# Spreading a state's C row over the partitions with one bf16 product instead of four fp32 transposes

## The chip, the cores and the metric

The kernel runs on one core of a Trainium2 chip. The metric is the device time of one launch in microseconds (us), the median of several runs. The engines are named as the profile names them: PE (TensorE), DVE (VectorE), ACT (ScalarE), POOL (GpSimd) and SP (SyncE, which here only issues DMAs). PEld is PE's weight load.

## What is computed

A block of two parts over x of shape 4 x 512 x 512: a selective scan (Mamba) gated by x, then a feed-forward part with ternary weights. Only the first part is touched by the change. Its core, per batch:

```
x_dbl = einsum('bdl,ed->bel', x, x_proj_w)
dt_low, Bm, Cm = split(x_dbl, [dt_rank, dt_rank + d_state], axis=1)
def step(state, inp):
    d, b, c, u = inp
    dA = exp(d[..., None] * A)
    state = state * dA + (d * u)[..., None] * b[:, None, :]
    y = einsum('bdn,bn->bd', state, c)
```

There are 16 states n, 512 channels d and 512 time steps l. In the kernel a channel is a partition, so state n of 128 channels is one 128 x 512 tile, and c for state n is one row of 512 numbers that all 128 partitions need: it has to be spread.

## The kernel before

The kernel is written engine by engine, with semaphores by hand; the order of the code of an engine is its order of execution, and a wait holds everything behind it on that engine.

**Prologue.** For each of the 4 batches, `project` and the convolution (`conv_start` on ACT, `taps` on DVE, `conv_sums` on POOL, `silu` on ACT) make u; `x_proj(b)` on PE and `rows_out(b)` on ACT make `rows[b]` (dt_low, B and C as 64 rows of 512, in tiles named zt, szT, zn, zt). SP stores rows 32 to 63 to `bc_rows` in HBM (`store_bc(b)`, L276), from where B rows (and some C rows) come back spread by DMA (`load_b`, L318, and `load_c`, L293). PE also transposes the same rows into `xdT` (`rows_transpose`, copied by `rows_copy` on DVE, L1311). Between these DVE makes sums of the weights (`w_abs`, L1303, and `w_means`, from L1316), statistics of x (`x_stats`, L1307) and one quarter of the ternary weights (`w_ternary(3)`, L1331), for which SP waits before it issues `load_b(0, (0,))`, since both use `b_bc`.

SP's list is fixed too: w_gate, x and w_up (4 MB each), then `store_u(0)`, `store_bc(0)`, `store_u(1)`, `store_bc(1)`, `store_u(2)`, `store_bc(2)`, then the loads of B for batch 0 with `store_u(3)` and pieces of x, then `store_bc(3)`, and so on. All go into one queue.

**Scan.** 16 stages s (4 batches x 4 groups of 128 channels) of 16 states n. For each state ACT makes exp (L1107), POOL makes du times B for two states at once (`times_b`, L850), DVE runs the scan (L1454), and the product with C is made either by POOL, for pairs, from C spread by DMA (`times_c`, L842), or by DVE for the "own" states (`times_c`, L1462), from C spread by PE into the PSUM tile pC (`c_bcast`, L477). PE then adds the product into pY by a transpose (`y_sum`, L483). Stages 0 to 3 have 12 own states each; the later ones 8 or 7. In all there are 133 calls of `c_bcast`, each of four transposes. In stages 4 to 15 the feed-forward of earlier token tiles runs beside the scan: PE's `gate_up` (L552), ACT's silu (L1060), DVE's `times_up` (L1406). In stages 0 to 3 pC has two banks for C, after that one.

**Tail.** After the last scan only the feed-forward of the last tiles is left; PE and ACT alternate there.

Of the kernel before, what the change touches and what calls it, by code (L numbers as in the profile page):

```python
# [6 lines left out]
BF16 = mybir.dt.bfloat16  # L7
# [5 lines left out]
P = 128  # L13
# [10 lines left out]
NPROJ = 64  # L24
BROW = 32
# [68 lines left out]
def by_pe(s, n):  # L94
# [11 lines left out]
    k_const k_acc k_lag2 k_tap k_conv k_u k_px k_xp k_rows k_tr k_xdT k_v k_dt k_st k_zs k_a  # L106
# [18 lines left out]
def build(nc, x, ctxT, g_x, g_f, w_in, w_conv, b_conv, w_xp, w_dt, b_dt, a_log, d_skip, w_gate, w_up, w_down,  # L125
          bc_rows, u_rows, out):
    with ExitStack() as stack:
# [3 lines left out]
        def ps(name, shape, dt=F32):  # L131
            return stack.enter_context(nc.psum_tensor(name, shape, dt))
# [82 lines left out]

        pA = ps("pA", [P, 2, 512])
# [56 lines left out]
        def _(sp):  # L273
            def store_bc(b):
                sp.wait_ge(S["k_rows"], b + 1)
                sp.dma_start(bc_rows[b], rows[b][BROW:NPROJ, :]).then_inc(S[f"c_bst{b}"], 16)  # L276

# [76 lines left out]
            sp.wait_ge(S["c_bst0"], 16)  # L354
# [14 lines left out]
            for b in range(1, BATCH):  # L369
                sp.wait_ge(S[f"c_bst{b}"], 16)  # L370
# [24 lines left out]
        def _(pe):  # L395
# [76 lines left out]
            def c_bcast(s, n):  # L472
                m = own(s).index(n)

                past(pe, S["s_mul"], OWN_AT[s] + m - (1 if s < PLAIN else 0))
                for k in range(NT):
                    mm = pe.transpose(c_bank(s, m)[:, k * P:(k + 1) * P],  # L477
                                      xdT[:, s // NT, k, NS + n:NS + n + 1].to_broadcast([P, P]), ident[:, :])
                mm.then_inc(S["s_cb"], 1)
# [296 lines left out]
        def _(gp):  # L776
# [13 lines left out]

            def conv_sums(first, last):
                for i in range(first, last):
                    gp.wait_ge(S["k_tap"], i + 1)
                    gp.wait_ge(S["k_acc"], 2 * i + 2)
                    gp.tensor_tensor(xc[i % 4][:, 1:L], xc[i % 4][:, 1:L], xb[i % 4][:, 1:L], ALU.add).then_inc(S["k_conv"], 1)  # L795
# [14 lines left out]
            w_round(1)  # L810
            conv_sums(12, 14)
# [3 lines left out]
            w_clip(3)  # L815

# [51 lines left out]
            for c in range(NDB):  # L868
                times_b(0, c)
# [58 lines left out]
        def _(act):  # L928
# [19 lines left out]
            def rows_out(b):  # L948

                act.wait_ge(S["k_xp"], b + 1)  # L950
                if b == 3:
                    act.wait_ge(S["c_bst0"], 16)
                    act.wait_ge(S["k_v"], NT)
                    act.wait_ge(S["k_tr"], 1)
                act.activation(rows[b], pT[:, :], ACT.Identity, bias=one_row[:, :]).then_inc(S["k_rows"], 1)
# [158 lines left out]
            def z_copy(s):  # L1114
                act.wait_ge(S["s_szp"], s + 1)
                past(act, S["s_x1"], s)
                if s == 0:
                    act.wait_ge(S["c_bst1"], 16)
                act.activation(szT[:, :], pT[:, :], ACT.Copy, scale=tgate[:, 0:1]).then_inc(S["s_szT"], 1)
# [22 lines left out]
            for s in range(PLAIN):  # L1142
                for n in range(NS):
                    if s * NS + n + 3 < PLAIN * NS + 2:
                        exponential(s * NS + n + 3)
                    if s == 0 and n == 3:
                        act.wait_ge(S["c_bst2"], 16)
                        act.wait_ge(S["k_xdT"], BATCH)
                        act.wait_ge(S["k_zs"], 4)
                        z_silu(0)  # L1150
                        act.wait_ge(S["c_bst3"], 16)
                        z_silu(1)
# [130 lines left out]
        def _(dve):  # L1283
# [44 lines left out]

            def w_ternary(c):
# [7 lines left out]
            dve.tensor_scalar(a_neg[:, :, :], a_raw[:, :, :], -1.0, None, ALU.mult)  # L1337
            w_abs(0, 0)
            taps(6)
# [5 lines left out]
            w_means(0)  # L1345
            taps(10)
# [6 lines left out]
            taps(14)  # L1353
            rows_copy(2)
# [5 lines left out]
            w_ternary(3)  # L1360
            w_abs(1, 0)
# [3 lines left out]
            w_abs(1, 3)  # L1365
            dve.wait_ge(S["c_ust"], 16 * BATCH)
# [230 lines left out]
```

## Time and profile before

| what | value |
|---|---|
| median of 3 runs | 621.03 us (620.51 to 621.07) |
| span of the profiled execution | 617.3 us |
| what lies around the span (median less span) | 3.7 us |
| DVE, POOL, ACT, PE busy, share of the span | 90%, 82%, 84%, 84% |

The span is from the first instruction to the last one in the profile; the profile gives no time of its own beside it, so the median stands in for it, and the difference of 3.7 us is taken as the same for both kernels. A busy share is an average over prologue, scan and tail, which have different limits.

### The profile page before, as it was taken

The page shows a single profiled execution, that of the slowest core. Times are in us where ns is not written, and L with a number is a line of the kernel's source. Part 1 is how long each engine was busy: PE and PEld are TensorE (multiplying, and loading weights), DVE is VectorE, ACT ScalarE, POOL GpSimd, SP SyncE. Part 2 cuts the span into 40 slices and gives each one's busy share as a digit, 9 for nine tenths or more (in the row PEclk, how much of TensorE's full clock was granted, in tenths as well). Part 3 has the DMA queues.
Part 4 walks back from the last instruction along what each step waited for, and adds up shares of the span by engine and source line. Part 5 has one row for each costly group of instructions (what it writes and reads, how often), then busy time and mean ns, then how long its engine had stood idle before and what let it go on. Part 6 is the DMA issues. An engine that isn't in the chain of part 4 may idle for free. (4 is left out here: it accounts for less than half of the span.)

```text
span 617.3 us, 9751 instructions
## 1 busy us (share of the span) xinstructions
PE 520.0 (84%) x3254; PEld 363.1 (59%) x3254; DVE 557.0 (90%) x766; ACT 519.0 (84%) x796; POOL 508.1 (82%) x286
## 2 busy tenths in 40 slices
PE   6999666757776888999879989998799898999996
PEld 2443355646664767676747666666467666655553
DVE  2899979999999899999899999998999999987564
ACT  4869788985998899899798999997988988768884
POOL 2568799999999899999999999999999999931000
PEclk9999768989699999999999999999999999999999
DMA  9992941620751010117501111175111110000001
GB/s 286 401 414 88 354 156 34 245 80 1 271 206 52 0 53 2 35 35 277 188 31 35 36 35 35 35 266 195 35 35 36 35 36 18 2 18 18 18 19 51
DMA packets 30420, 64.25 MB, mean 104 GB/s; under 512 B 3729, under 2 KB 11921, under 8 KB 27554
## 3 DMA queue, kind: packets, MB, share of 16 engines
q1 hardware_dynamic: 30370, 63.63, 29.1%
q8 instruction: 26, 0.43, 0.3%
q14 instruction: 24, 0.20, 0.1%
HBM read 55.49 MB, written 8.13 MB: 103 GB/s over the span
## 5 line engine op out<-in xcount | busy, mean ns | idle before, releaser
L850 POOL TENSOR_TENSOR area_s<-area_s,b_bc 128x1024 f32<-128x1024 f32 x117 | 275.0, 2363 | 13.8 <-DVE u_all L1454 9.2
L483 PE MATMUL pY<-ident,area_s 128*128 128x128 f32 x532 | 87.6, 290 | 56.6 <-DVE area_s L1462 56.6
L552 PE MATMUL pG<-wq_gu,area_f 128*128 128x512 fp8e4 x448 | 107.9, 379 | 4.0 <-ACT area_f L1052 2.9
L1454 DVE TENSOR_TENSOR_SCAN area_s<-pA,area_s 128x512 f32<-128x512 f32 x88 | 105.2, 1207 | 5.1 <-ACT pA L1107 4.4
L483 PEld LDWEIGHTS pY<-ident,area_s 128*128 128x128 f32 x532 | 61.6, 146 | 78.0 <-DVE area_s L1462 70.5
L1107 ACT ACTIVATE pA<-dt_all,a_neg 128x512 f32<-128x512 f32 x145 | 97.7, 682 | 10.7 <-DVE area_s L1454 5.9
L842 POOL TENSOR_TENSOR u_all<-u_all 128x1024 f32<-128x1024 f32 x44 | 103.9, 2361 | 0.2 <-DMA u_all<-bc_rows 0.2
L1462 DVE TENSOR_TENSOR area_s<-area_s,pC 128x512 f32<-128x512 f32 x133 | 87.9, 664 | 0.8 <-DVE area_s L1454 0.5
L477 PE MATMUL pC<-ident,xdT 128*128 128x128 f32 x532 | 83.2, 283 | 3.6 <-DVE area_s L1462 2.3
L477 PEld LDWEIGHTS pC<-ident,xdT 128*128 128x128 f32 x532 | 64.3, 143 | 8.9 <-DVE area_s L1462 7.4
L552 PEld LDWEIGHTS pG<-wq_gu,area_f 128*128 128x128 bf16 x448 | 41.7, 98 | 47.1 <-ACT area_f L1052 3.9
L596 PE MATMUL pT<-wq_dn,area_f 128*128 128x512 fp8e4 x240 | 57.5, 379 | 0.0
L483 PE MATMUL pY<-ident,u_all 128*128 128x128 f32 x352 | 48.7, 284 | 2.0 <-POOL u_all L842 2.0
L831 POOL TENSOR_TENSOR sm<-sm,neg_half 128x1 f32<-128x1 f32 x16 | 8.8, 552 | 44.9 <-ACT sm L1070 33.7
L483 PEld LDWEIGHTS pY<-ident,u_all 128*128 128x128 f32 x352 | 42.2, 147 | 5.3 <-POOL u_all L842 2.4
L1406 DVE TENSOR_TENSOR area_f<-area_f,pG 128x512 f32<-128x512 f32 x52 | 34.6, 678 | 8.3 <-PE pG L552 6.3
L1107 ACT ACTIVATE pC<-dt_all,a_neg 128x512 f32<-128x512 f32 x57 | 38.9, 683 | 3.4 <-DVE u_all L1454 2.4
L1454 DVE TENSOR_TENSOR_SCAN u_all<-pA,area_s 128x512 f32<-128x512 f32 x33 | 39.6, 1212 | 0.1
L1060 ACT ACTIVATE area_f<-pG,sm 128x512 f32<-128x512 f32 x52 | 34.4, 685 | 4.3 <-PE pG L552 3.3
L583 PE MATMUL pG<-ident,area_f 128*128 128x128 f32 x176 | 24.0, 278 | 15.9 <-ACT area_f L1093 13.1
L795 POOL TENSOR_TENSOR area_s<-area_s 128x511 f32<-128x511 f32 x16 | 20.0, 1269 | 20.0 <-DVE area_s L1293 20.0
L1454 DVE TENSOR_TENSOR_SCAN area_s<-pC,area_s 128x512 f32<-128x512 f32 x29 | 35.0, 1207 | 1.4 <-ACT pC L1107 1.4
(211 smaller groups left out, 1143.9 us busy)
## 6 DMA issues: line engine op xcount, KB each, us to landing
b_bc<-bc_rows SPq DMA_DIRECT2D x14, 1024.0 KB, 6.5
area_s<-x SPq DMA_DIRECT2D x32, 256.0 KB, 2.9
u_all<-bc_rows SPq DMA_DIRECT2D x14, 512.0 KB, 5.9
b_bc<-w_gate SPq DMA_DIRECT2D x1, 4096.0 KB, 14.5
dt_all<-x SPq DMA_DIRECT2D x1, 4096.0 KB, 24.8
area_f<-w_up SPq DMA_DIRECT2D x1, 4096.0 KB, 34.2
area_f<-w_down SPq DMA_DIRECT2D x1, 4096.0 KB, 14.4
out<-area_f SPq DMA_DIRECT2D x16, 256.0 KB, 2.1
```

The costliest lines, as they stand in the source:

```text
L477: mm = pe.transpose(c_bank(s, m)[:, k * P:(k + 1) * P], xdT[:, s // NT, k, NS + n:NS + n + 1].to_broadcast([P, P]), ident[:, :])
L483: mm = pe.matmul(pY[:, k * P:(k + 1) * P], src[:, k * P:(k + 1) * P], ident[:, :], is_transpose=True, start=(first and k == 0), stop=(last ...
L552: mm = pe.matmul(bank, xqT[t % 2][:, k, :], wq_gu[:, k, m, c * GW:(c + 1) * GW], start=(k == 0), stop=(k == NT - 1))
L583: mm = pe.transpose(banks[r % 2][:, k * P:(k + 1) * P], h_of(t)[:, (4 * r + k) * P:(4 * r + k + 1) * P], ident[:, :])
L596: mm = pe.matmul(pT[:, :], hqT[t % 2][:, k, :], wq_dn[:, k, :], start=(k == 0), stop=(k == FK - 1))
L842: gp.tensor_tensor(hp[j], hp[j], c_bc[j], ALU.mult).then_inc(S["s_pmul"], 1)
L850: gp.tensor_tensor(db[c % NDB], du[s % 2].rearrange("p (a l) -> p a l", a=1).to_broadcast([P, CH, L]), b_bc[:, CH * c:CH * c + CH, :], ALU ...
L1060: act.activation(h_of(t)[:, c * GW:(c + 1) * GW], bank, ACT.Silu, scale=col(CS[t % 2])).then_inc(S["f_silu"], 1)
L1107: act.activation(exp_bank(s, n), dt_all[:, s, :], ACT.Exp, scale=a_neg[:, s % NT, n:n + 1]).then_inc(S["s_exp"], 1)
L1406: dve.tensor_tensor(chunk, chunk, bank, ALU.mult).then_inc(S["f_h"], 1)
L1454: dve.tensor_tensor_scan(h, at, dbu, 0.0, ALU.mult, ALU.add).then_inc(S["s_scan"], 1)
L1462: dve.tensor_tensor(p_st[i % NH], h_st[i % NH], c_bank(s, m), ALU.mult).then_inc(S["s_mul"], 1)
```

## The change

`c_bcast` becomes one product. The stationary operand is one column of a constant bf16 selector `sel_c`, repeated 128 times; the moving operand is `c_pk`, a bf16 tile whose partitions hold the C rows in three parts (high, middle and low bits), 48 partitions for an even batch from partition 0 and 48 for an odd one from partition 64. A product with ones and zeros, accumulated in fp32, gives the sum of the three parts, so C itself.

To make `c_pk`, four steps per batch are added: `store_bc` issues three more DMAs, each a copy of the 16 C rows from SBUF to SBUF (`c_raw`), on the same semaphore as the store; DVE's `c_cut` waits for all four and runs two scalar_tensor_tensor over 48 x 512 that leave the residuals; POOL's `c_pack` copies the upper halves to `c_pk`. POOL also clears two tiles and builds the selector at the start, and DVE builds two masks. Every wait on a `c_bst` semaphore now asks for 64 where it asked for 16.

```diff
+                if b == 0:
+                    sp.wait_ge(S["k_sel"], 1)
+                for i in range(PARTS):
+                    at = C_AT * (b % 2) + NS * i
+                    sp.dma_start(c_raw[at:at + NS, b // 2, :], rows[b][BROW + NS:NPROJ, :]).then_inc(S[f"c_bst{b}"], 16)
...
-                for k in range(NT):
-                    mm = pe.transpose(c_bank(s, m)[:, k * P:(k + 1) * P],
-                                      xdT[:, s // NT, k, NS + n:NS + n + 1].to_broadcast([P, P]), ident[:, :])
-                mm.then_inc(S["s_cb"], 1)
+                b = s // NT
+                pe.wait_ge(S["k_cpk"], 2 * (b // 2) + 2)
+                pe.matmul(c_bank(s, m), sel_c[:, b % 2, n:n + 1].to_broadcast([P, P]), c_pk[:, b // 2, :],
+                          start=True, stop=True).then_inc(S["s_cb"], 1)
...
+            gp.memset(c_raw[:, :, :], 0.0).then_inc(S["k_sel"], 1)
+            gp.memset(c_pk[:, :, :], 0.0).then_inc(S["k_sel"], 1)
+            part = [ident[:, :].rearrange("p (h k) -> p h k", h=2)[:, :, NS * i:NS * i + NS] for i in range(PARTS)]
+            gp.tensor_tensor(sel_c[:, :, :], part[0], part[1], ALU.add).then_inc(S["k_sel"], 1)
+            gp.wait_ge(S["k_sel"], 3)
+            gp.tensor_tensor(sel_c[:, :, :], sel_c[:, :, :], part[2], ALU.add).then_inc(S["k_sel"], 1)
+
+            def c_pack(b):
+                at = C_AT * (b % 2)
+                gp.wait_ge(S["k_cut"], b + 1)
+                gp.tensor_copy(c_pk[at:at + PARTS * NS, b // 2, :], c_top[at:at + PARTS * NS, b // 2, :]).then_inc(S["k_cpk"], 1)
...
             w_round(1)
+            c_pack(0)
             conv_sums(12, 14)
...
             w_clip(3)
+            gp.wait_ge(S["k_clip"], 1)
+            c_pack(1)
+            gp.wait_ge(S["k_cpk"], 2)
...
-            for c in range(NDB):
-                times_b(0, c)
+            times_b(0, 0)
+            times_b(0, 1)
+            c_pack(2)
+            times_b(0, 2)
+            times_b(0, 3)
+            gp.wait_ge(S["s_dbu"], NDB)
+            c_pack(3)
+            gp.wait_ge(S["k_cpk"], BATCH)
...
+            def c_cut(b):
+
+                at, h = C_AT * (b % 2), b // 2
+                dve.wait_ge(S[f"c_bst{b}"], 16 * (PARTS + 1))
+                dve.wait_ge(S["k_mask"], PARTS - 1)
+                if b == 0:
+                    dve.wait_ge(S["k_sel"], 2)
+                for i in range(PARTS - 1):
+                    past(dve, S["k_half"], b + 1 if i else 0)
+                    part = c_raw[at:at + PARTS * NS, h, :]
+                    dve.scalar_tensor_tensor(out=part, in0=c_top[at:at + PARTS * NS, h, :], scalar=low_parts[at:at + PARTS * NS, i:i + 1],
+                                             in1=part, op0=ALU.mult, op1=ALU.subtract).then_inc(S["k_cut" if i else "k_half"], 1)
...
             w_means(0)
+            c_cut(0)
             taps(10)
...
             taps(14)
+            c_cut(1)
             rows_copy(2)
...
             w_ternary(3)
+            c_cut(2)
             w_abs(1, 0)
             w_abs(1, 1)
             rows_copy(3)
             w_abs(1, 2)
             w_abs(1, 3)
+            c_cut(3)
             dve.wait_ge(S["c_ust"], 16 * BATCH)
...
-    nc = bacc.Bacc("TRN2", target_bir_lowering=False, num_devices=1)
+    nc = bacc.Bacc("TRN2", target_bir_lowering=False, num_devices=1, dynamic_dma_scratch_size=4096)
```

The last line makes room in SBUF; every DMA of the program is issued by SP on the queue q1 (hardware_dynamic).

Three places in the order of the instructions. First DVE in the middle of the prologue, from `w_means(0)` through `taps(10)`; before:

```order
L1303 TENSOR_REDUCE w_sum<-b_bc 128x1 x2
L1316 TENSOR_REDUCE w_mean<-pY 128x1
L1318 TENSOR_SCALAR w_mean<-w_mean 128x1
L1320 RECIPROCAL w_inv<-w_mean 128x1
L1323 TENSOR_SCALAR k_gate<-w_mean 128x1
L1293 SCALAR_TENSOR_TENSOR area_s<-pC,w_cv,area_s 128x510 x2
L1293 SCALAR_TENSOR_TENSOR area_s<-pC,w_cv,area_s 128x509 x2
```

and in the changed kernel, whose line numbers are higher by some tens:

```order
L1339 TENSOR_REDUCE w_sum<-b_bc 128x1 x2
L1352 TENSOR_REDUCE w_mean<-pY 128x1
L1354 TENSOR_SCALAR w_mean<-w_mean 128x1
L1356 RECIPROCAL w_inv<-w_mean 128x1
L1359 TENSOR_SCALAR k_gate<-w_mean 128x1
L1375 SCALAR_TENSOR_TENSOR c_raw<-c_raw,low_parts 48x512 x2
L1329 SCALAR_TENSOR_TENSOR area_s<-pC,w_cv,area_s 128x510 x2
L1329 SCALAR_TENSOR_TENSOR area_s<-pC,w_cv,area_s 128x509 x2
```

`c_cut(0)`, with its wait for four DMAs, stands ahead of the convolution of batches 2 and 3.

Second DVE at the end of the prologue, where the first scans are (the order names a scan SCALAR_TENSOR_TENSOR); before:

```order
L1331 TENSOR_SCALAR wq_gu<-b_bc 128x2048
L1303 TENSOR_REDUCE w_sum<-area_f 128x1 x2
L1311 COPY xdT<-pY 128x128
L1303 TENSOR_REDUCE w_sum<-area_f 128x1 x2
L1454 SCALAR_TENSOR_TENSOR area_s<-pA,area_s 128x512 x2
```

and changed:

```order
L1380 TENSOR_SCALAR wq_gu<-b_bc 128x2048
L1375 SCALAR_TENSOR_TENSOR c_raw<-c_raw,low_parts 48x512 x2
L1339 TENSOR_REDUCE w_sum<-area_f 128x1 x2
L1347 COPY xdT<-pY 128x128
L1339 TENSOR_REDUCE w_sum<-area_f 128x1 x2
L1375 SCALAR_TENSOR_TENSOR c_raw<-c_raw,low_parts 48x512 x2
L1511 SCALAR_TENSOR_TENSOR area_s<-pA,area_s 128x512 x2
```

`c_cut(3)` is the last thing ahead of the first scan.

Third SP's queue in the same stretch, from the first load of B for batch 0; before:

```order
L318 DMA b_bc<-bc_rows 128x2048
L281 DMA u_rows<-u_all 128x4x512
L318 DMA b_bc<-bc_rows 128x2048
L305 DMA area_s<-x 128x512 x2
L310 DMA area_s<-x 128x4x128
L318 DMA b_bc<-bc_rows 128x2048 x2
L276 DMA bc_rows<-zt 32x512
L310 DMA area_s<-x 128x4x128
```

and changed:

```order
L332 DMA b_bc<-bc_rows 128x2048
L295 DMA u_rows<-u_all 128x4x512
L332 DMA b_bc<-bc_rows 128x2048
L319 DMA area_s<-x 128x512 x2
L324 DMA area_s<-x 128x4x128
L332 DMA b_bc<-bc_rows 128x2048 x2
L285 DMA bc_rows<-zt 32x512
L290 DMA c_raw<-zt 16x512 x3
L324 DMA area_s<-x 128x4x128
```

The three copies for batch 3 stand behind its store, and both behind four loads of B, `store_u(3)` and three loads of x.

## Rows read from the trace of the kernel before

**Rows 1.** The page's busy totals: us, share of the span, instructions.

```profile
PE 520.0 (84%) x3254; PEld 363.1 (59%) x3254; DVE 557.0 (90%) x766; ACT 519.0 (84%) x796; POOL 508.1 (82%) x286
```

**Rows 2.** Busy time of the engines by stretch: start:end, length, each engine's busy us, PEclk.

```profile
90.00:540.00 450.00, 377.00 (x2661) 288.26 (x2662) 437.95 (x564) 394.92 (x608) 439.16 (x227) 0.98 0.23 80
...
97.00:151.00 54.00, 35.19 (x258) 30.21 (x258) 53.80 (x66) 42.93 (x55) 53.38 (x26) 0.94 0.29 103
...
70.00:85.00 15.00, 7.29 (x32) 5.45 (x31) 12.06 (x16) 11.04 (x13) 14.07 (x7) 0.52 0.92 351
299.00:330.00 31.00, 24.86 (x177) 18.52 (x176) 30.15 (x46) 25.76 (x43) 29.99 (x17) 1.00 0.25 77
```

**Rows 3.** Waits of DVE, 90 to 540 us: total us, times, longest.

```profile
DVE area_f L1406 <- PE pG L552: 5.1, 7, 1.5
DVE area_s L1454 <- ACT pA L1107: 2.4, 5, 1.1
DVE area_s L1454 <- ACT pC L1107: 1.4, 3, 0.8
```

**Rows 4.** Longest waits of POOL (90 to 535 us) and of PE (whole span).

```profile
POOL area_s L850 <- DVE u_all L1454: 9.2, 12, 2.5
...
PE pY L483 <- DVE area_s L1462: 56.6, 56, 3.5
```

**Rows 5.** DVE's timeline in the prologue: start, us, instruction, [idle before, releaser].

```profile
38.98 2.71 DVE L1293 SCALAR_TENSOR_TENSOR area_s<-pC,w_cv,area_s 128x510 f32<-128x510 f32 x4
...
51.37 0.29 DVE L1311 COPY xdT<-pY 128x128 f32<-128x128 f32 x1 [1.28 <-PE pY L425]
...
59.31 1.20 DVE L1331 TENSOR_SCALAR wq_gu<-b_bc 128x2048 fp8e4<-128x2048 f32 x1
...
70.14 2.34 DVE L1454 TENSOR_TENSOR_SCAN area_s<-pA,area_s 128x512 f32<-128x512 f32 x2 [0.66 <-DMA u_rows<-u_all]
```

**Rows 6.** Stores of C and B rows, 20:30 and 50:85: KB, us to landing.

```profile
bc_rows<-zt SPq DMA_DIRECT2D x1, 64.0 KB, 17.6
...
bc_rows<-zn SPq DMA_DIRECT2D x1, 64.0 KB, 3.3
bc_rows<-zt SPq DMA_DIRECT2D x1, 64.0 KB, 13.0
```

**Rows 7.** SP's timeline: stores of batches 0, 2, 3, and the first B load.

```profile
27.17 1.31 SPq L276 DMA_DIRECT2D bc_rows<-zt  x1
...
50.01 0.32 SPq L276 DMA_DIRECT2D bc_rows<-zn  x1
60.54 0.34 SPq L318 DMA_DIRECT2D b_bc<-bc_rows  x1
...
66.72 1.89 SPq L276 DMA_DIRECT2D bc_rows<-zt  x1
```

**Rows 8.** Duration of DVE's scalar_tensor_tensor in the prologue: ns min/median/max.

```profile
L1293 DVE SCALAR_TENSOR_TENSOR area_s<-pC,w_cv,area_s x16: 732/738/749, 14.4 to 49.4; 128x510 f32<-128x510 f32 x8, 128x509 f32<-128x509 f32 x8
```

**Rows 9.** ACT and DVE timelines in stage 0.

```profile
79.76 0.82 ACT L1112 ACTIVATE zt<-area_s,z_nmr,z_rstd 128x512 f32<-128x512 f32 x1 [2.06 <-DMA bc_rows<-zt]
...
82.61 1.22 DVE L1454 TENSOR_TENSOR_SCAN u_all<-pG,area_s 128x512 f32<-128x512 f32 x1 [1.53 <-ACT pG L1107]
85.11 2.34 DVE L1454 TENSOR_TENSOR_SCAN area_s<-pA,area_s 128x512 f32<-128x512 f32 x2 [1.28 <-ACT pA L1107]
...
88.53 1.22 DVE L1454 TENSOR_TENSOR_SCAN area_s<-pG,area_s 128x512 f32<-128x512 f32 x1 [0.49 <-ACT pG L1107]
```

**Rows 10.** POOL's last work on the weights in the prologue.

```profile
54.50 1.89 POOL L805 TENSOR_SCALAR b_bc<-b_bc 128x2048 f32<-128x2048 f32 x1
```

**Rows 11.** PE's timeline in stage 4: four transposes, then eight products.

```profile
198.69 0.65 PE L477 MATMUL pC<-ident,xdT 128*128 128x128 f32 x4 [0.62 <-DVE area_s L1462]
199.17 1.89 PE L552 MATMUL pG<-wq_gu,area_f 128*128 128x512 fp8e4 x8
```

**Rows 12.** DVE in stage 4, waiting for the product that follows.

```profile
203.27 0.69 DVE L1406 TENSOR_TENSOR area_f<-area_f,pG 128x512 f32<-128x512 f32 x1 [1.52 <-PE pG L552]
```

More of the change, by code:

```diff
@@ L24 @@
 NPROJ = 64
+PARTS = 3
+C_AT = 64
 BROW = 32
@@ L105 @@
 SEMAPHORES = """c_a c_in c_small c_ctx0 c_ctx1 c_ctx2 c_ctx3 c_x c_w c_bst0 c_bst1 c_bst2 c_bst3 c_ust c_g0 c_g1 c_g2
-    k_const k_acc k_lag2 k_tap k_conv k_u k_px k_xp k_rows k_tr k_xdT k_v k_dt k_st k_zs k_a
+    k_const k_acc k_lag2 k_tap k_conv k_u k_px k_xp k_rows k_tr k_xdT k_v k_dt k_st k_zs k_a k_sel k_mask k_half k_cut k_cpk
     k_abs k_abv k_ws k_wm k_p1 k_p3 k_clip
@@ L214, in build @@
         z_buf = [zn, zt]
+        c_raw = sb("c_raw", [P, 2, L])
+        c_top = c_raw[:, :, :].bitcast(BF16).rearrange("p h (l two) -> p h l two", two=2)[:, :, :, 1]
+        c_pk = sb("c_pk", [P, 2, L], BF16)
+        sel_c = sb("sel_c", [P, 2, NS], BF16)
+        low_parts = sb("low_parts", [P, PARTS - 1])
         pA = ps("pA", [P, 2, 512])
@@ L353, in _ @@
             sp.wait_ge(S["k_p3"], NW)
-            sp.wait_ge(S["c_bst0"], 16)
+            sp.wait_ge(S["c_bst0"], 16 * (PARTS + 1))
             load_b(0, (0,))
@@ L369, in _ @@
             for b in range(1, BATCH):
-                sp.wait_ge(S[f"c_bst{b}"], 16)
+                sp.wait_ge(S[f"c_bst{b}"], 16 * (PARTS + 1))
             load_z(2)
@@ L951, in rows_out @@
                 if b == 3:
-                    act.wait_ge(S["c_bst0"], 16)
+                    act.wait_ge(S["c_bst0"], 16 * (PARTS + 1))
                     act.wait_ge(S["k_v"], NT)
@@ L1117, in z_copy @@
                 if s == 0:
-                    act.wait_ge(S["c_bst1"], 16)
+                    act.wait_ge(S["c_bst1"], 16 * (PARTS + 1))
                 act.activation(szT[:, :], pT[:, :], ACT.Copy, scale=tgate[:, 0:1]).then_inc(S["s_szT"], 1)
@@ L1146, in _ @@
                     if s == 0 and n == 3:
-                        act.wait_ge(S["c_bst2"], 16)
+                        act.wait_ge(S["c_bst2"], 16 * (PARTS + 1))
                         act.wait_ge(S["k_xdT"], BATCH)
@@ L1150, in _ @@
                         z_silu(0)
-                        act.wait_ge(S["c_bst3"], 16)
+                        act.wait_ge(S["c_bst3"], 16 * (PARTS + 1))
                         z_silu(1)
@@ L1337, in _ @@
             dve.tensor_scalar(a_neg[:, :, :], a_raw[:, :, :], -1.0, None, ALU.mult)
+            dve.wait_ge(S["k_const"], 7)
             w_abs(0, 0)
+            for i in range(PARTS - 1):
+                halves = ident[:, :].rearrange("p (h k) -> p h k", h=2)
+                dve.tensor_reduce(low_parts[:, i:i + 1], halves[:, :, NS * (i + 1):NS * PARTS], mybir.AxisListType.XY, ALU.add).then_inc(S["k_mask"], 1)
             taps(6)
```

## Prediction

> **What bounds the kernel now.** I read the busy totals first, then busy time by stretch, then the waits of the engines that are fullest, and last the timelines of the places that the change touches.
>
> DVE has the most work, PE as much as ACT [rows 1]. By stretch it is plainer: from 90 to 540 us, nearly the whole scan, DVE is busy 438.0 of 450 us and POOL 439.2, PE 377.0 [rows 2]. Which of the two full engines leads is told by the waits: POOL waits 9.2 us for DVE's scans [rows 4], and no wait of DVE for POOL stands in the list, whose entries are 5.1 us for PE's gate and up products and 2.4 and 1.4 us for ACT's exponentials [rows 3]. So in the scan DVE sets the pace, and the most that anything off DVE can give there is 5.1 + 2.4 + 1.4 = 8.9 us. PE is no bound: its largest wait is 56.6 us, and it is for DVE's products, ahead of `y_sum` [rows 4].
>
> The prologue is DVE's too. From `taps(10)` at 38.98 us to the first scan at 70.14 us its timeline has two idle pieces, 1.28 us (for PE's transposes) and 0.66 us (for the last store of u) [rows 5]; everything else is work in a fixed order. A step put into that list, or a wait, moves the first scan, and the scan moves with it.
>
> **What is removed.** 133 times four transposes on PE. Four of them take 199.17 - 198.69, about 0.45 us start to start; eight products 128x512 run 1.73 us, 0.22 each [rows 11]. One bf16 product 128x512 in place of four transposes thus frees 0.23 us of PE, 133 x 0.23 = 31 us in all. The row is of fp8 against bf16; bf16 against bf16 is bounded above by what it replaces (gain 0) and below by that 0.22, and the tile shape makes me take 0.22.
>
> What of it reaches the end? In stages 0 to 3 nothing: DVE was busy 53.8 of 54 us in two of them [rows 2]. In stages 4 to 15 only where PE, not DVE, was last. The longest such wait is 1.52 us before `times_up` at 203.27 [rows 12]; on the way to it PE makes `c_bcast(11)` at 198.69 and then two gates [rows 11], so 0.23 us comes off there and in the two like stages (8 and 12). In the other stages the chain into `times_up` runs from ACT's silu or DVE's product through `y_sum(10)`, with no broadcast in between. In the tail one broadcast (state 15) stands between DVE's last two products, 0.2 us. Sum: 3 x 0.23 + 0.2, about **-1.0 us**; bounds 0 and -8.9.
>
> **What is added on POOL.** Two clears and two small sums at the start end long before its first convolution sum. `c_pack(0)` and `c_pack(1)` are each one copy of 512 columns: POOL's pass over 2048 columns took 1.89 us [rows 10], so 0.5, at most 1.3 if it costs as much as a product of 512. Both lie before 56.4 us of the old time, and what needs POOL there is `w_ternary(3)` at 59.31 [rows 5]: 2.9 us of cover, so **0**; with the cover gone it would be 0.5 to 1.3. `c_pack(2)` and `c_pack(3)` lie among products that run ahead of a first scan that is now late: 0.
>
> **What is added on DVE and SP, batch 0.** `c_cut(0)` waits for the store and three copies. The store was issued at 27.17 [rows 7] and took 17.6 us to land [rows 6], since 12 MB of weights and x stand ahead of it: 44.8 us. DVE comes to the wait when taps(10) began, 38.98 [rows 5], plus 0.3 for the masks, two reductions of one short row each (an estimate, off the path, since it only shortens the wait). The copies (32 KB each) stand right behind the store in the queue. No row shows such a copy; bounds are 0, carried along by the full queue, and 3.3 us, the landing of a store in an empty queue [rows 6]. I take 0.4, near zero, because the queue is full. Each cut is two dependent instructions of 0.74 us [rows 8], 1.5 us. So `taps(10)` starts at 44.8 + 0.4 + 1.5 = 46.7 in place of 38.98: 7.7 us late. Queued behind the wait are taps(10) to taps(14), for which POOL's sums, ACT's silu, PE's `x_proj(2)` and `x_proj(3)` wait in turn; all move along.
>
> **Batch 1.** Its store stands ahead of batch 2's, which was issued at 50.01 [rows 7] and landed 3.3 us later [rows 6]; DVE is there at 57.8. No wait, 1.5 us of work, which fills the idle 1.28 us before the copy at 51.37 [rows 5]: the list is now **8.0 us** late. So is `w_ternary(3)`, and with it SP's first load of B, which waited for it until 60.54 [rows 7], and SP's list behind.
>
> **Batches 2 and 3.** `c_cut(2)` waits for nothing (its store, moved along by 8 us, lands by 61.3) and its 1.5 us lie ahead of the next wait. `c_cut(3)` needs the store of batch 3: issued at 66.72 [rows 7], landed 13.0 us later [rows 6], 79.7 us, behind some 5.7 MB of B, u and x. ACT shows the same moment: it waited for that store until 79.76 [rows 9]. In the new kernel that is 79.7 + 8.0, the copies 0.4, the cut 1.5: the first scan starts at **89.6 us** in place of 70.14, **+19.5 us**. Nothing hides it: DVE has no other work in its list, the scan is DVE's.
>
> **What comes back.** In stage 0 DVE idled 1.53 + 1.28 + 0.49 us for exponentials, because ACT stood 2.06 us before `z_silu(1)` waiting for that same store [rows 9]. The store has now landed long before, ACT is through 2.06 us earlier, and the first idle piece goes; of the others a part. I take **-1.8**, bounds 0 and -2.1.
>
> Sum against the profile's span: 617.3 + 19.5 - 1.8 - 1.0 = 634.0; with the 3.7 us around it **637.7 us**, 2.7% over 621.03.
>
> **A rule weighed.** PE does less from here on, so its clock matters. From 97 to 151 us the only products that are no transposes are the eight of two `y_skip`, of 258 instructions, and the granted clock was 0.94, the 2.4 GHz level for nearly all of it; from 70 to 85 us, after PE had idled, it was 0.52, the 1.2 GHz level [rows 2]. So here a PE that only transposes holds the high clock. The Trainium skill (TensorE: Matmul & The Clock Gate, Part 4: PE-mode transpose) says that transpose-mode does not count as PE activity for the clock. By that rule the change could only help the clock and the clock rival below would have no chance; the trace speaks against the rule, so it keeps one.
>
> **Rivals.**
> 1. *The copies are slow*: each group lands 3.3 us after its store, as if the queue were empty, at both places: 2 x 2.9 = 5.8 more, 643.5. For it: small pieces on 16 partitions only; against: a full queue hides latency.
> 2. *One of the two waits is not there*: for instance batch 0's store lands sooner than before, or the work behind it catches up. Without the 8.0 us: 629.7. Against: one store, one landing, and DVE's list has no slack.
> 3. *The clock falls* in the stages where PE has least to do. From 299 to 330 us PE was busy 24.9 of 31 us [rows 2]; less seven broadcasts at 0.23 it is 23.3. If a third of that ran at 1.2 GHz, 7.8 us of work would take 15.6 in 10.3 us of time, 5.3 late; in two such stages 10.6: 648.3. Against: two stages with PE busy 35 of 54 us held 0.94.
> 4. *Other side: the small transfers are not held by the queue.* Decides at `c_cut`: if the store and copies of batch 0 land by 39.4 and those of batch 3 by the time DVE gets there (about 73). Then only work is added: 4 x 1.5 + 0.3 less the two idle pieces 1.9 gives 4.4, ACT's wait gives 1.8, and PE's relief between 1.0 and 8.9: from +1.6 to -6.3, 614.7 to 622.6. Faster only if the relief passes about 3.8. Against: 17.6 and 13.0 us to landing [rows 6].
>
> **How the numbers follow.** Forecast 0.65 (its own band 635 to 640.5); rival 1 0.10; rival 2 0.14; rival 3 0.05; rival 4 0.06, of which 0.04 faster and 0.02 within 0.2%, about what a measurement of this kernel can tell from no change. Range 629 to 644.5: forecast, rivals 1 and 2, 0.89, which allows for terms that are off by some us. Chances: faster 0.04, same 0.02, slower 0.94.
>
> **What would show it.** On DVE: an idle piece of about 6 us before the first cut, released by a DMA to `c_raw`; a second of about 9 us before the last cut; the first scan near 89.6 us. In stage 0 no wait of ACT for the store. From 90 us after that DVE's idle time as before, less about 1 us; POOL's wait for DVE not smaller. PE busy down by about 30 us, its waits for DVE longer by as much. Clock about as before in stages 4 to 15. It is wrong if the first scan starts before 80 us, or if DVE's waits for PE in the scan fall by more than 3 us.

## The result, and the profile after

The changed kernel takes 643.77 us (641.29 to 644.89) beside 620.77 us of the kernel before (620.1 to 621.07): ratio 1.0373, 95% interval 1.0355 to 1.0391, so 23 us slower. 637.7 was forecast, 16.7 us slower; the time lies inside the range (629 to 644.5), 0.7 us from its upper end, and the size was 6 us short.

The page of the changed kernel, its totals and DVE's and the clock's line of tenths, beside [rows 1]:

```profile
span 641.7 us, 9081 instructions
...
PE 500.1 (78%) x2814; PEld 322.4 (50%) x2855; DVE 568.8 (89%) x776; ACT 518.3 (81%) x796; POOL 513.0 (80%) x294
...
DVE  2859939999999989999899999998999999987664
...
PEclk9998955868859899999999999999999999999999
```

The span grew by 24.4 us (617.3 before), the median time by 23.0. The two differ because the span of 617.3 us seems to be that of an execution 1.9 us faster than the median of 621.03: in the changed kernel and in all ten runs below the time is 1.8 us above the span of the same execution, not the 3.7 us that were taken.

PE's total is 20 us lower and DVE's 12 us higher. PE's is not to be taken at its face: the trace has the weight loads of all 133 bf16 products, but only 92 of the products themselves, so some 9 to 16 us of PE's work may be missing from it (an estimate, 41 products at the 0.22 to 0.38 us of those that are there). DVE's tenths show where the time went: besides the start it has two dips, in slices 3 and 6 (each slice is 16 us), and from there on it is full until the tail.

DVE's timeline in the prologue of the changed kernel (start, us, instruction, idle before and releaser), which answers to [rows 5]:

```profile
39.36 0.15 DVE L1359 TENSOR_SCALAR k_gate<-w_mean 128x1 f32<-128x1 f32 x1
45.43 1.52 DVE L1375 SCALAR_TENSOR_TENSOR c_raw<-c_raw,low_parts 48x512 f32<-48x512 bf16 x2 [5.92 <-DMA c_raw<-zt]
46.88 2.70 DVE L1329 SCALAR_TENSOR_TENSOR area_s<-pC,w_cv,area_s 128x510 f32<-128x510 f32 x4
...
56.52 2.06 DVE L1329 SCALAR_TENSOR_TENSOR area_s<-pC,w_cv,area_s 128x510 f32<-128x510 f32 x3 [0.50 <-ACT area_s L978]
58.60 7.06 DVE L1375 SCALAR_TENSOR_TENSOR c_raw<-c_raw,low_parts 48x512 f32<-48x512 bf16 x2
65.70 0.29 DVE L1347 COPY xdT<-pY 128x128 f32<-128x128 f32 x1
...
73.76 1.19 DVE L1380 TENSOR_SCALAR wq_gu<-b_bc 128x2048 fp8e4<-128x2048 f32 x1
74.87 1.51 DVE L1375 SCALAR_TENSOR_TENSOR c_raw<-c_raw,low_parts 48x512 f32<-48x512 bf16 x2
...
95.36 1.54 DVE L1375 SCALAR_TENSOR_TENSOR c_raw<-c_raw,low_parts 48x512 f32<-48x512 bf16 x2 [10.00 <-DMA c_raw<-zt]
96.93 2.34 DVE L1511 TENSOR_TENSOR_SCAN area_s<-pA,area_s 128x512 f32<-128x512 f32 x2
```

The two waits that were forecast are there, 5.92 us (about 6) and 10.00 us (about 9), each released by a copy to `c_raw`. The first scan starts at 96.93 us; 70.14 was the old time and 89.6 the forecast. And there is a row that was not forecast: the two instructions of `c_cut(1)` take 7.06 us, while those of the other three cuts take 1.51 to 1.54.

What ran on POOL in that time (same kernel, POOL's timeline):

```profile
58.39 2.49 POOL L821 TENSOR_TENSOR area_s<-area_s 128x511 f32<-128x511 f32 x2
60.86 1.97 POOL L826 TENSOR_SCALAR b_bc<-b_bc,w_inv 128x2048 f32<-128x2048 f32 x1
62.92 2.21 POOL L831 TENSOR_SCALAR b_bc<-b_bc 128x2048 f32<-128x2048 f32 x1
```

POOL had no pause longer than 0.1 us from 58.4 to 65.1; DVE's pair ended at 65.66, 0.5 us after it. In the old kernel the last of these, 1.89 us there [rows 10], ended at 56.4 with DVE at other work.

The idle 0.50 us before 56.52 was not forecast either. It begins on PE. Its eight products for the convolution of one unit, and the granted clock (the number behind POOL's) where they ran, in the kernel before:

```profile
42.12 3.70 PE L402 MATMUL pC<-area_s 128*128 128x512 f32 x8
...
42.00:46.00 4.00, 4.00 (x13) 1.90 (x12) 4.00 (x7) 3.66 (x7) 4.00 (x4) 1.00 1.03 401
```

and in the changed one, with the instruction of ACT behind them:

```profile
48.98 6.11 PE L416 MATMUL pC<-area_s 128*128 128x512 f32 x8 [6.34 <-DVE area_s L1329]
...
50.00:54.00 4.00, 4.00 (x6) 1.66 (x5) 4.00 (x8) 2.46 (x4) 4.00 (x5) 0.52 0.25 93
...
55.13 0.78 ACT L977 ACTIVATE area_s<-pC,b_cv,w_cv 128x512 f32<-128x512 f32 x1 [0.98 <-PE pC L416]
```

While DVE stood for the copies, PE had nothing to do for 6.34 us; after that the granted clock was 0.52, the 1.2 GHz level, and the same eight products took 6.11 us in place of 3.70. ACT waited for them, and DVE for ACT.

From the first scan on the changed kernel goes on as the one before did. The last scan-time step of the feed-forward on DVE (the output at 541.18 us of the old timeline) stands at 565.77 us: +24.6, of the first scan's +26.8; 2.2 us were given back in between. DVE's longest waits from 115 to 565 us are those of [rows 3]:

```profile
DVE area_f L1463 <- PE pG L566: 4.6, 7, 1.3
DVE area_s L1511 <- ACT pA L1143: 2.4, 5, 1.1
DVE area_s L1511 <- ACT pC L1143: 1.4, 3, 0.8
```

and PE has traded work for waiting, 79.9 us against the 56.6 of [rows 4]; 13.5 of it is one wait for the late first scan, and the time of the products that the trace lacks counts as waiting too:

```profile
PE pY L497 <- DVE area_s L1519: 79.9, 69, 13.5
```

### The profile page after: what moved, and what is told of

Its sections match the earlier page's. It is cut to its first block and busy times, and to the rows that moved or that the text cites. A ratio compares the mean times of both kernels' runs of the same rounds, so it can differ in the third digit from the quotient of the medians.

```text
span 641.7 us, 9081 instructions
## 1 busy us (share of the span) xinstructions
PE 500.1 (78%) x2814; PEld 322.4 (50%) x2855; DVE 568.8 (89%) x776; ACT 518.3 (81%) x796; POOL 513.0 (80%) x294
## 5 line engine op out<-in xcount | busy, mean ns | idle before, releaser
L497 PE MATMUL pY<-ident,area_s 128*128 128x128 f32 x532 | 91.9, 300 | 80.1 <-DVE area_s L1519 79.9
L497 PEld LDWEIGHTS pY<-ident,area_s 128*128 128x128 f32 x532 | 64.6, 151 | 111.5 <-DVE area_s L1519 100.9
L497 PEld LDWEIGHTS pY<-ident,u_all 128*128 128x128 f32 x352 | 43.6, 149 | 5.0 <-POOL u_all L872 1.5
L861 POOL TENSOR_TENSOR sm<-sm,neg_half 128x1 f32<-128x1 f32 x16 | 8.8, 552 | 44.8 <-ACT sm L1106 33.5
L492 PE MATMUL pC<-c_pk,sel_c 128*128 128x512 bf16 x92 | 38.1, 426 | 2.4 <-DVE area_s L1519 2.0
L610 PEld LDWEIGHTS pT<-wq_dn,area_f 128*128 128x128 bf16 x240 | 23.5, 98 | 23.0
```

Of the source, the lines that this page charges most:

```text
L492: pe.matmul(c_bank(s, m), sel_c[:, b % 2, n:n + 1].to_broadcast([P, P]), c_pk[:, b // 2, :], start=True, stop=True).then_inc(S["s_cb"], 1)
L497: mm = pe.matmul(pY[:, k * P:(k + 1) * P], src[:, k * P:(k + 1) * P], ident[:, :], is_transpose=True, start=(first and k == 0), stop=(last ...
L610: mm = pe.matmul(pT[:, :], hqT[t % 2][:, k, :], wq_dn[:, k, :], start=(k == 0), stop=(k == FK - 1))
```

## The experiments

Theory after the result: all of the loss is a later first scan, made of two waits for the copies, of DVE's own work for the cuts, and of `c_cut(1)` held up by POOL; PE's relief is worth nothing, since DVE sets the pace. Times are medians; each ratio is to the kernel before, run on the same chip (620.4 us, for the last two runs 620.6).

### PE's relief alone

```diff
-                for i in range(PARTS):
-                    at = C_AT * (b % 2) + NS * i
-                    sp.dma_start(c_raw[at:at + NS, b // 2, :], rows[b][BROW + NS:NPROJ, :]).then_inc(S[f"c_bst{b}"], 16)
...
-            c_cut(0)
...
-            c_pack(0)
...
-            gp.memset(c_pk[:, :, :], 0.0).then_inc(S["k_sel"], 1)
+            gp.memset(c_pk[:, :, :], 0.37).then_inc(S["k_sel"], 1)
```

(and so for all four cuts and packs)

> The bf16 product in place of the four transposes, without the copies, the cuts and the packs: c_pk holds the constant 0.37, so the C of DVE's own states is left out. The masks and the selector stay. This is the change's gain on PE alone. Theory (DVE sets the pace, PE's relief is worth about 1.0 us, the two mask reductions cost DVE 0.4): 620.4 us against 621.0 for the kernel before. Rival (PE's relief removes DVE's waits for PE and ACT in the scan, up to 8.9 us): about 614 to 617. Second rival (less PE work lowers PE's clock, and that costs time): above 622.

Measured: 620.32 us, ratio 1.0002 (0.9993 to 1.0010). The profile has PE at 355 us of work in 90 to 540 us against 377 before [rows 2], so 22 us less, though here too 41 of the 133 products aren't in the trace, and the first scan 0.33 us later for the masks. Its windows, 90 to 540 us:

```profile
90.00:540.00 450.00, 355.02 (x2247) 248.45 (x2286) 437.49 (x564) 393.22 (x607) 438.89 (x226) 0.95 0.23 80
```

DVE's 437.49 against 437.95 before: the same work in the same time. PE's granted clock fell from 0.98 to 0.95 over the stretch. One row may show for it: DVE waits 0.33 us for PE in stage 1, where it had no wait, and that stage is 0.6 us longer; the median has no trace of it. Both rivals fall: no gain of some us, no loss by the clock. With the masks in it the relief comes to between 0.4 us faster and 0.6 us slower.

### The first wait taken away

```diff
             w_means(0)
-            c_cut(0)
             taps(10)
...
             taps(14)
-            c_cut(1)
             rows_copy(2)
...
             w_ternary(3)
+            c_cut(0)
+            c_cut(1)
             c_cut(2)
...
+            gp.wait_ge(S["k_zs"], 4)
+            c_pack(0)
+            c_pack(1)
+            gp.wait_ge(S["k_cpk"], 2)
             times_b(0, 0)
```

> The changed kernel with c_cut(0) and c_cut(1) moved on DVE from before taps(10) and after taps(14) to just behind w_ternary(3), and c_pack(0), c_pack(1) moved on POOL to before times_b(0, 0). Theory (the 5.9 us wait of c_cut(0), its 1.5 us and the 7.1 us of c_cut(1) delayed all that follows, while their new place lies before a wait for a DMA anyway): the first scan starts near 82.9 us in place of 96.9, 14 us less, 629.8 us. All three cuts there take 1.5 us each, since POOL is nearly idle. Rival (the prologue's delay is made good elsewhere): the first scan moves by less than 5 us, 639 or more. Rival (c_cut(1) is slow by itself, not by what runs beside it): it takes 7 us in its new place too.

Measured: 630.84 us, ratio 1.0160 (1.0140 to 1.0180). DVE's timeline:

```profile
61.21 4.64 DVE L1375 SCALAR_TENSOR_TENSOR c_raw<-c_raw,low_parts 48x512 f32<-48x512 bf16 x6
81.46 1.54 DVE L1375 SCALAR_TENSOR_TENSOR c_raw<-c_raw,low_parts 48x512 f32<-48x512 bf16 x2 [6.63 <-DMA c_raw<-zt]
83.03 2.34 DVE L1511 TENSOR_TENSOR_SCAN area_s<-pA,area_s 128x512 f32<-128x512 f32 x2
```

The first scan at 83.03 where 82.9 was expected, the three cuts at 4.64 us together: `c_cut(1)` is not slow by itself. POOL was not idle beside them, as the expectation had it, but at work on tiles of 16 columns (POOL's timeline):

```profile
61.50 3.25 POOL L889 TENSOR_TENSOR z_rstd<-z_rstd,neg_half 128x16 f32<-128x16 f32 x1
```

So POOL being busy is not enough to hold a cut up. The kernel is 12.9 us faster than the changed one (643.8): the delay of the prologue went into the end nearly whole.

### Both waits taken away

Here `c_cut(3)` also goes, into stage 1:

```diff
             w_abs(1, 3)
-            c_cut(3)
...
                     if s == 0 and n == 1:
                         w_means(1)
+                    if s == 1 and n == 2:
+                        c_cut(3)
...
+                    if s == 1 and n == 12:
+                        gp.wait_ge(S["s_dbu"], db_count(s + 1, 1))
+                        c_pack(3)
+                        gp.wait_ge(S["k_cpk"], BATCH)
```

> As e2_cuts01_late, and c_cut(3) moved into stage 1 of the scan, its c_pack(3) behind it on POOL in the same stage, so that no DMA is waited for ahead of the first scan. Theory (the second wait, 10.0 us, was pure delay): the first scan starts near 74.3 us (70.1 plus 0.4 for the masks and 4.5 for three cuts, less what was idle), 4.2 us later than in the kernel before. What c_cut(3) costs in stage 1, where POOL is never idle, tells the contention apart: if DVE with two SBUF inputs is held up by a busy POOL, it takes about 7 us and the kernel 631 us; if not, 1.5 us and 625.7 us.

Measured: 623.23 us, ratio 1.0045 (1.0031 to 1.0059). The first scan starts at 75.27 us (74.3 expected), and the moved cut is

```profile
108.26 1.54 DVE L1376 SCALAR_TENSOR_TENSOR c_raw<-c_raw,low_parts 48x512 f32<-48x512 bf16 x2
```

Under both prices expected, and it tells nothing on contention: POOL's product ended at 108.4, 0.2 us after the cut began, and POOL then stood until 111.13. So the cut had met a pause. What is left over the kernel before is 2.9 us by the medians and 4.2 by the two spans (621.5 and 617.3). By the spans: the first scan is 5.1 us later, stage 0 is 1.5 us shorter (27.74 us from its first scan to that of stage 1, where it was 29.27), stage 1 with the cut 1.8 longer, and 1.2 come back later.

### The second wait alone

(`c_pack(3)` stands where it stood in the version before.)

```diff
-            c_cut(3)
...
+                    if s == 1 and n == 2:
+                        c_cut(3)
```

> The changed kernel with c_cut(3) moved into stage 1 of the scan and c_pack(3) behind it, all else as changed: only the second wait (10.0 us) and its 1.5 us are taken out from ahead of the first scan. Theory (waits add up, each as pure delay): DVE is free at 85.4 us, the first scan starts there, 11.5 us earlier than in the changed kernel; c_cut(3) costs 1.5 in stage 1, where it met a pause of POOL before; ACT may stand a little for the store of batch 3 again (about 1): 634.5 us. With e2 (-13 us) and both together (-20.5 us) this closes a square: if the waits hid each other, the two single steps would not add up to the double one. Rival (the second wait only stands in for another, as the B rows or the last store of u): the first scan stays above 90 us.

Measured: 637.49 us, ratio 1.0259 (1.0231 to 1.0287). The first scan is at 85.69 us, as expected (85.4), so the wait stood for nothing else. But the time is 3 us above the expectation. Part of it is ACT's old wait, back and longer, and with it DVE's three idle pieces of stage 0, 3.6 us in place of 1.5 in the changed kernel: stage 0 takes 29.5 us in place of 27.7, 1.8 more, where about 1 was allowed. ACT's and DVE's timelines:

```profile
95.58 0.82 ACT L1149 ACTIVATE zt<-area_s,z_nmr,z_rstd 128x512 f32<-128x512 f32 x1 [2.34 <-DMA c_raw<-zt]
...
98.43 1.22 DVE L1511 TENSOR_TENSOR_SCAN u_all<-pG,area_s 128x512 f32<-128x512 f32 x1 [1.81 <-ACT pG L1144]
```

Another 0.3 is the first scan, and 0.4 is stage 1, 1.9 us longer for a cut of 1.5. The remaining 1.5 us I can't place.

The square: first wait alone -12.9, second alone -6.3, both -20.5 (from 643.8). At the end the steps nearly add up (-19.2), but that is two things in balance. At the first scan they don't: -13.9, -11.2, and both -21.7, 3.4 us less than their sum. With the first wait gone the second is 6.63 us in place of 10.00, since the cuts that were moved, 3.1 us of work, now take up part of its time. So the waits do hide each other in part, and ACT's wait, which comes back when only the second is taken away, makes up for it in the time.

### One input of the slow cut from PSUM

```diff
-                    dve.scalar_tensor_tensor(out=part, in0=c_top[at:at + PARTS * NS, h, :],
+                    if b == 1:
+                        dve.wait_ge(S["k_v"], 1)
+                    dve.scalar_tensor_tensor(out=part, in0=pG[0][at:at + PARTS * NS, :] if b == 1 else c_top[at:at + PARTS * NS, h, :],
```

> The changed kernel, where c_cut(1) alone reads its first input from a PSUM bank (pG0) in place of c_raw's upper halves, so that only one of its two tensor inputs comes from SBUF; the middle and low parts of batch 1's C are left out (other numbers stand there). Same place, same size, same work of POOL beside it. Theory (two SBUF inputs on DVE beside a busy POOL is what made 1.5 us into 7.1 us): c_cut(1) takes 1.5 us, the kernel 638.2 us. Rival (any DVE instruction there is held up, or bf16 reads with a step of two are slow): it stays at 7 us or in between, 643.8 us.

(PE and ACT also wait for this cut before they use that bank again.) Measured: 638.45 us, ratio 1.0295 (1.0276 to 1.0315), 5.3 us below the changed kernel. DVE's timeline:

```profile
57.95 1.55 DVE L1381 SCALAR_TENSOR_TENSOR c_raw<-pG,low_parts,c_raw 48x512 f32<-48x512 f32 x2
```

Same place, same length, same neighbours: 1.55 us in place of 7.06. So DVE's work there is not slow as such. The input read from PSUM is also fp32 with a step of one, where it was bf16 with a step of two. The other cuts, bf16 too and 1.5 us, show that such a read isn't slow by itself; that it is the memory and not the type which lets POOL hold the cut up is not separated, since no instruction with two fp32 inputs in SBUF ran beside a busy POOL.

### The last cut beside a POOL without a pause

Against the version with both waits taken away (`c_pack(3)` moves along, behind product 14 of stage 2):

```diff
-                    if s == 1 and n == 2:
+                    if s == 2 and n == 9:
                         c_cut(3)
```

> As e4_both_moved, but c_cut(3) stands in stage 2 after scan 9, where POOL runs products of 1024 columns without a pause from 140 to 160 us, and not in stage 1, where it met a pause of 2.7 us. Theory (a scalar_tensor_tensor with both tensor inputs in SBUF gets through only where POOL leaves a gap): the two instructions take 5 to 7 us in place of 1.5 and the kernel 4 to 5 us more than e4's 623.2, 627.5 us. Rival (only POOL's instructions with one tensor input, as ran beside c_cut(1), hold DVE up; products of two tensors don't): 1.5 us, 623.2 us.

Measured: 626.70 us, ratio 1.0104 (1.0087 to 1.0120), 3.5 us above the version with the cut in stage 1. DVE's and POOL's timelines:

```profile
142.67 4.04 DVE L1376 SCALAR_TENSOR_TENSOR c_raw<-c_raw,low_parts 48x512 f32<-48x512 bf16 x2
...
138.72 4.68 POOL L876 TENSOR_TENSOR area_s<-area_s,b_bc 128x1024 f32<-128x1024 f32 x2
143.35 2.80 POOL L868 TENSOR_TENSOR u_all<-u_all 128x1024 f32<-128x1024 f32 x1
146.12 1.71 POOL L863 TENSOR_TENSOR area_s<-dt_all,u_all 128x512 f32<-128x512 f32 x1
```

4.04 us in place of 1.54; 5 to 7 was expected. POOL pays too: 2.80 and 1.71 us for products that take 2.36 and 1.26 elsewhere. So products of two tensors on POOL hold DVE up as well. The place costs more than the cut shows: from the first scan of stage 2 to that of stage 3 it is 32.2 us, where it is 26.5 in the version that this one is compared with, 5.7 more; in stage 1 the same cut made 1.8.

The theory that a cut gets through only where POOL leaves a gap fails, though: POOL's rows follow each other without one. What the rows do show is when each of the two instructions ended, and it is the same in all four kernels where cuts were held up (the last column counts the ends of POOL's instructions in between that did not let it through):

| kernel | instruction of a cut, from to | a POOL instruction ended | difference | POOL's ends passed by |
|---|---|---|---|---|
| changed | 58.60 to 63.37 | 62.83 | 0.54 | 2 |
| changed | 63.40 to 65.67 | 65.12 | 0.55 | 0 |
| second wait alone | 58.70 to 63.78 | 63.23 | 0.55 | 3 |
| second wait alone | 63.81 to 66.07 | 65.53 | 0.54 | 0 |
| this one | 142.67 to 143.96 | 143.41 | 0.55 | 0 |
| this one | 143.99 to 146.71 | 146.16 | 0.55 | 0 |
| the next one | 59.44 to 60.66 | 60.11 | 0.55 | 0 |
| the next one | 60.70 to 62.35 | 61.80 | 0.55 | 0 |
| the next one | 82.08 to 83.70 | 83.15 | 0.55 | 0 |
| the next one | 83.73 to 89.31 | 88.76 | 0.55 | 2 |

An instruction that was held up is thus not slow: it stands until one of POOL's instructions ends and is done 0.55 us later. Where an instruction of POOL starts then, it takes 0.3 to 0.5 us longer than usual. Why some let two or three of POOL's ends go by, no run shows.

### The store of batch 3 first

```diff
             store_bc(2)
+            store_bc(3)
             sp.wait_ge(S["k_p3"], NW)
...
             load_b(0, (2, 3))
-            store_bc(3)
```

> The changed kernel with one move in SP's list: store_bc(3), with its three copies, ahead of the first load of B for batch 0 in place of behind the fourth. rows(3) is there at 68.6 us and SP stood until 75.0 for w_ternary(3), so the move holds nothing up. Theory (the second wait is queueing behind 5.7 MB, nothing else): store and copies land near 73 us, c_cut(3) doesn't wait, the first scan starts at 86.9 us in place of 96.9: 633.8 us. Rival (the copies themselves are slow, or c_cut(3) waits for something else too): the first scan stays above 90 us.

Measured: 638.57 us, ratio 1.0293 (1.0269 to 1.0318). Half of the expectation held: `c_cut(3)` waits for no DMA any more. But it now runs beside POOL's first products, and

```profile
82.08 7.24 DVE L1375 SCALAR_TENSOR_TENSOR c_raw<-c_raw,low_parts 48x512 f32<-48x512 bf16 x2
89.34 2.34 DVE L1511 TENSOR_TENSOR_SCAN area_s<-pA,area_s 128x512 f32<-128x512 f32 x2
```

5.7 us of the 10 came back as contention. That the first scan still starts at 89.34, near the 86.9 expected, is luck: in this kernel `c_cut(1)` took 2.91 us, where the changed one has 7.06 and the one with only `c_cut(3)` moved 7.37. By the table above the pair has no fixed price beside a busy POOL, since it depends on which of POOL's ends lets it in. The rest of what the time is above the expectation (4.8 us, of which the first scan makes 2.4) was not followed.

### The same move in the kernel before

> The kernel before with the same move alone: store_bc(3) ahead of load_b(0, (0,)). ACT stood 2.06 us for that store in stage 0 and DVE then idled 1.53 us for an exponential. Theory: ACT's wait goes, DVE's first idle piece in stage 0 goes, the scan ends 1.5 to 1.8 us earlier, 618.7 us, faster than both kernels. Rival (POOL or the later loads of B, which now stand behind 64 KB more, take over): no change, 620.4 us.

Measured: 619.47 us, ratio 0.9985 (0.9973 to 0.9996). ACT's wait is gone, but a wait shows in stage 0 that was hidden (DVE):

```profile
83.26 2.34 DVE L1454 TENSOR_TENSOR_SCAN area_s<-pA,area_s 128x512 f32<-128x512 f32 x2 [0.73 <-ACT pA L1107]
87.52 0.69 DVE L1462 TENSOR_TENSOR area_s<-area_s,pC 128x512 f32<-128x512 f32 x1 [1.93 <-issue]
```

The product waits for its C in pC. PE's timeline shows why it is late:

```profile
84.61 1.97 PE L483 MATMUL pY<-ident,u_all 128*128 128x128 f32 x8 [2.04 <-POOL u_all L842]
86.37 1.06 PE L477 MATMUL pC<-ident,xdT 128*128 128x128 f32 x4
```

PE stands for POOL's first product with C, and the broadcast is queued behind it, at the low clock (0.50 in that stretch, after PE had idled). A second measurement, beside the next kernel:

> A second measurement of e8, beside e9 on the same chip: about 619.5 us, 0.9 below the kernel before. The profile should again show a wait of 1.9 us of DVE before a product with C in stage 0, behind which stands PE's broadcast of 1.1 us at the low clock, itself behind the pooled sum that waits for POOL.

It gave 619.33 us, ratio 0.9994 (0.9982 to 1.0005), with the same wait, 1.88 us. One interval excludes no change and the other doesn't; that this version beats the kernel before by its expected 1.5 us is not shown. The spans don't show it either, 617.7 and 617.9 us against 617.3: stage 0 is 0.7 us shorter, and stages 1 and 2 together 0.8 longer, with 0.46 and 0.36 us of new waits before a product with C.

### PE's relief where PE is last

> e1 (bf16 product, no preparation, C of DVE's own states left out) with the move of e8. If PE's relief is worth something only where PE is last, then here: the wait of 1.9 us that e8 shows in stage 0 shrinks by 0.6 to 0.7, what one bf16 product saves on four transposes at the low clock. With 0.3 for the masks: 619.2 us, against e8's 619.5. Rival (relief is worth nothing anywhere): the wait stays at 1.9 us and the time is e8's plus 0.3.

The edit is the sum of the first one and the last. Measured: 618.60 us, ratio 0.9978 (0.9964 to 0.9992). The wait of 1.93 us is now

```profile
86.86 0.69 DVE L1506 TENSOR_TENSOR area_s<-area_s,pC 128x512 f32<-128x512 f32 x1 [1.27 <-issue]
```

0.66 us shorter, as was expected of one bf16 product against four transposes at the low clock, and the waits of 0.46 and 0.36 us are gone too. So here the rows show the relief arriving at DVE, about 1.5 us in all, which is also what the two spans differ by (616.3 and 617.7 or 617.9). By the medians it is 0.7 us on the same chip, and the two intervals overlap, so in the time the gain of the product alone is not shown; that of both steps together over the kernel before is (0.5 to 2.2 us). The preparation that would make it right costs 23.

## Why the prediction was right, and where it was short

- **DVE sets the pace of the scan, POOL has no say, PE none.** Right for this kernel. The relief with the masks in it measured 0.0 us (0.4 faster to 0.6 slower); -1.0 for the relief was in the sum (bounds 0 and -8.9), and 0.3 for the masks was taken as hidden by the wait, which it was in the full change. Of the three places priced at 0.23 us each one came out so: the wait before `times_up` in stage 4 is 1.26 us in place of 1.52, those of stages 8 and 12 only 0.04 and 0.05 shorter, and one that was not counted 0.22. Together DVE's waits for these products are 4.6 us against 5.1 in [rows 3]. PE's total was to fall by about 30 us and fell by 20, with 41 products missing from it, so by less. The price of a product was right: two in a row at the granted clock 1.00 start 0.21 us apart. The kernel with the store moved shows the limit of the statement: once the wait for the store is gone, DVE does wait for PE in stages 0 to 2.
- **The first wait.** Right: store landed at 44.6 us (44.8), copies 0.8 us behind it (0.4), `taps(10)` at 46.88 (46.7).
- **Batch 1: "No wait, 1.5 us of work".** This is the term that failed: 7.06 us. I took the duration from a row whose first input lies in PSUM [rows 8] and applied it to an instruction with both in SBUF, in a stretch where POOL has no pause. It makes 5.6 of the 7.3 us by which the first scan came later than forecast. Another 0.5 is the wait for ACT behind PE's products at the low clock. That a DVE that stands lets PE go idle and lose its clock was not in the sum at all; where the granted clock was 0.75 in that stretch (`c_cut(1)` from PSUM) this wait is not there.
- **The second wait.** Right in mechanism and size: store of batch 3 landed 20.4 us after `w_ternary(3)` began in both kernels (79.7 - 59.31 and 94.1 - 73.76). The copies came 1.2 us behind it, not 0.4: 0.8 us more.
- **What comes back in stage 0.** -1.8 was forecast. Stage 0 gave back 1.5, and from the first scan to the end of the scan it is 2.2 us. The second wait taken away brought ACT's wait back, which shows the cause.
- **Sum.** 634.0 us of span were forecast, 641.7 measured. Of these 7.7 us, 7.3 stand at the first scan: 5.6 (the cut beside POOL), 0.5 (PE's clock), 0.2 (first wait), 0.8 (copies) and 0.2 that I can't place. The other 0.4 is what was given back (2.4 in all, where 2.8 was forecast). In the time the miss is only 6.1, and that is luck: the 3.7 us added to the span should have been 1.8. With 1.8 the forecast would have been 635.8, and 8.0 short.
- **The rule weighed.** From 97 to 151 us of the kernel before, 18 of the 258 instructions are no transposes (sixteen for the products of `y_skip`, where I counted eight, and two for a sum of weights), and the granted clock is 0.94 [rows 2]. The Trainium skill (TensorE: Matmul & The Clock Gate, Part 4: PE-mode transpose) says that transpose-mode does not count as PE activity for the clock. The row speaks against that. The changed kernel adds nothing to it. Its granted clock in the stages after stage 0 is lower (the number behind POOL's):

```profile
117.00:143.00 26.00, 16.86 (x90) 12.32 (x91) 25.54 (x30) 23.08 (x27) 24.23 (x12) 0.77 0.23 79
```

  where it was 0.94 with the transposes in place [rows 2]. But the kernel before with only the store moved, all transposes in place, has in stages 1 and 2

```profile
99.00:125.00 26.00, 17.80 (x125) 15.97 (x124) 25.54 (x30) 22.39 (x26) 25.92 (x13) 0.87 0.51 183
125.00:152.00 27.00, 19.50 (x130) 16.69 (x128) 26.54 (x35) 19.34 (x27) 26.75 (x14) 0.81 0.09 30
```

  and the last kernel, the same with bf16 products for those transposes,

```profile
99.00:125.00 26.00, 15.71 (x90) 11.10 (x89) 25.95 (x30) 21.75 (x26) 25.92 (x13) 0.87 0.52 182
125.00:152.00 27.00, 16.75 (x91) 11.49 (x90) 26.82 (x35) 20.65 (x27) 26.92 (x14) 0.81 0.10 30
```

  The same clock with and without them: whether the transposes that were taken out counted for it is not shown.
- **Rivals.** Slow copies: a little (0.4 and 0.8 us more than taken, of 2.9). One wait missing: no. The clock falls in the scan: it did in stages 0 to 4, with no time clearly lost by it (stages 1 to 3 take 78.9 us and took 78.6), and in stages 5 to 15 it is 1.00 as before; the clock did cost 0.5 us, but in the prologue. Small transfers not held by the queue: no, 17.3 and 12.5 us to landing, as before.

## What to carry to other kernels

An engine that is full in a fixed order turns nearly every wait placed in its list into time at the end, however small the step is that waits; what a step costs there depends on where the data is at that moment, so follow the DMA queue ahead of it and not the size of the transfer. Work taken off an engine that is waiting for the full one is worth next to nothing: look first at who waits for whom, and look again when a wait has been removed, since another may stand behind it. And a duration is only good for another instruction if its operands lie in the same memories and the same neighbours run.

## What the runs showed of the hardware that I had not expected

- A scalar_tensor_tensor of DVE with both tensor inputs in SBUF can be held up while POOL works on wide tiles. A pair takes 1.51 to 1.55 us beside an idle POOL and also beside POOL's instruction on 128x16, but 7.06, 7.37 and 2.91 (beside POOL's convolution sums and passes over weights), 7.24 (beside its products of 1024 columns at the end of the prologue) and 4.04 us (in stage 2). With one input in PSUM, and fp32 in place of bf16, it takes 1.55 in the same place. One instruction of a pair alone took 4.76 us where 0.74 is usual. Each of the ten that were held up ended 0.54 or 0.55 us after one of POOL's instructions ended.
- The Trainium skill (VectorE: DVE Perf Modes, Two Vector instructions with no wait between them) says that an instruction with two SBUF tensor inputs reads one of them through a second SBUF read interface, shared with GpSimd. The traces agree for POOL's wide instructions (7.06 us against 1.55); that 3.25 us of POOL on 128x16 held up none of the cuts beside it (0.73 to 0.75 us each) is not explained by it. Nearly all of DVE's work in the scan of this kernel has one input in PSUM, which fits with POOL running beside it.
- POOL is slowed as well, but less: 2.21 us for 1.89, 2.80 for 2.36, 1.71 for 1.26.
- Copies of 16 partitions from SBUF to SBUF, queued behind a store in a full queue, landed 0.8 and 1.2 us after it.
- After 6.34 us in which PE had nothing to do, its granted clock was 0.52 and the same eight products took 6.11 us in place of 3.70.
